# A fused four-stage attention and adapter kernel: three of its TensorE transposes cut into 64-row halves, laid side by side around a group of score products

## The chip, the cores and the metric

The kernel runs on one core of one Trainium2 chip. The metric is the device time of one execution in microseconds (us).

## The reference

For each of 32 samples (256 tokens, 256 features) four residual stages follow each other. Cut to what matters:

```
# stage 1: attention, 16 heads of 16 features; key 0..255 from x, one more key per token from itself
q = (side + b_self) @ Wq + bq;  k = (x + b_prev) @ Wk + bk;  v = x @ Wv + bv
score = q . k / 4, masked beyond the sample's length;  self = q . k_own / 4
w = softmax([score, self]);  attn = w[:-1] @ v + w[-1] * v_own;  x1 = x + attn @ Wo + bo
# stage 2: adapter chosen per sample, layer norm
h = relu(x1 @ W1[id] + b1[id]);  x2 = x1 + layernorm(x1 + h @ W2[id] + b2[id]) * gamma[id] + beta[id]
# stage 3: linear layer chosen per sample
x3 = x2 + x2 @ W3[id].T + b3[id]
# stage 4: pooling with one softmax row per token under a mask chosen per sample
s = tanh(x3 @ W4 + b4) @ v4;  p = softmax(mask(s));  out = x3 + p @ x3 / count
```

## The kernel before

The 32 samples go through a software pipeline: step t computes projections of sample t+2, row maxima of the scores of t+1, the exponentials and weighted values of t, the end of attention of t-1, adapter and linear layer of t-2, pooling of t-3. Steps 6 to 27 are a hardware loop of two steps an iteration; the others are written out. Each engine has its own program in a fixed order, written by hand; semaphores order the engines among each other. There is no scheduler.

TensorE's program of a step is built around eight calls of `scores(pair)`, called S0 to S7 below. Each call issues eight products of 64 rows by 128 columns with 256 moving columns: four write score columns into ST (L584; ScalarE exponentiates them, two "units" a call), four write score rows into SN (L588; VectorE takes the maxima, two units a call). The two kinds lie on different halves of the array's rows (`lo_`, `hi_`) and run side by side. Before it starts, `scores(pair)` waits until the maxima and exponentials of the calls before have been taken. Between the calls stand the other products, almost all of the full array, 128 rows by 128 columns:

- between S1 and S2: `own_keys()` (12 products into bank 2, read by VectorE's `products`, L1386), then `h` (6 products into bank 1);
- between S2 and S3: `queries_back(0)` and `queries_back(1)` (L615): four 128x128 transposes each, of the weighted values `pvt` to token rows in banks `num0` (0) and `num1` (1); then `queries()`;
- between S4 and S5: `own_scores()`, `values("v", ...)`;
- between S5 and S6: `turn(pT, pe3)` and `turn(aT, att)` (L489): four 128x128 transposes each, of the pooling probabilities `pe3` (in `soft`) into bank 1 and of the attention rows `att` (in `nv`) into bank 2; then `weighted(0, ...)` (L563), of 32-column tiles;
- between S6 and S7: `x2T`, the transposes of the normed rows `yn`, then `pool` and `wo`.

A transpose is a product with the data as the stationary operand (its load is a LDWEIGHTS) and the identity (in `fixed`) as the moving one.

`free(name)` waits until the last user of a bank has been read: it walks back through the list `PIECES` (position, name, sample, bank) to the last piece on the same bank, and waits for that piece's entry in `READER`:

```
"h": (("hf", 1, 1),), ... "num0": (("nv", 2, 1),), "num1": (("nv", 2, 2),),
```

So `num1`, on bank 1 behind `h`, waits for `hf`. That is the second of two ScalarE reads of h (L1164 writes `hst`, L1166 writes `hf`). ScalarE's order around it is: units 2 and 3 (L1052), the copy of `pvt` (L1028), the copy of `xs`, `hst`, `hf`, units 4 and 5. Around `pe3` it is: `keys_out` (`kf`), the copy `lwp`, units 8 and 9, the two exponentials of `pe3` with a read of their sums (L1188), the copy `vaug`, units 10 and 11, the copies `p3T` and `aT`, the two `yn` activations (L1206), units 12 and 13. ScalarE and VectorE, like TensorE, take their programs in order.

Of the kernel before, what the change touches and what calls it, by code (L numbers as in the profile page):

```python
# [40 lines left out]
B, S, D = 32, 256, 256  # L41
H, DH = 16, 16
P = 128
NC2 = D // P
# [18 lines left out]


PIECES = [
# [5 lines left out]
]  # L71
# [3 lines left out]
def done(b, per=1, nth=None):  # L75

    nth = per if nth is None else nth
    if isinstance(b, int):
        return 0 if b < 0 else B * per if b >= B else b * per + nth
    return b * per + nth  # L80
# [14 lines left out]
def block4(nc: bass.Bass, x, xsT, lens, ids, wq, wk, wv, wo, wad, lw, lwT, lb, fixed_d, early_d, kidx_d,  # L95
           pmask_d, out):
    ctx = ExitStack()
    with ctx:
# [8 lines left out]
        def sem(name):  # L107
            if name not in sems:
                sems[name] = ctx.enter_context(nc.semaphore(name))
            return sems[name]  # L110
# [7 lines left out]
        ss = [[sb(f"ss{i}{r}", [P, NC2, S], F32R) for r in range(2)] for i in range(2)]  # L118
# [16 lines left out]
        pvt = sb("pvt", [P, 4, S])  # L135
# [3 lines left out]
        att = nv  # L139
# [49 lines left out]
        ident = fixed[:, 2 * H:2 * H + P]  # L189
# [63 lines left out]
        def place(name, t):  # L253

            if isinstance(t, int) and (t, name) in LATE:
                return LATE[t, name][0]
            return place("pool", t) if name == "pool1" else bank[name]
# [40 lines left out]
        def folding(t):  # L298

            return isinstance(t, int) and 0 <= t < 2  # L300
# [174 lines left out]
        def _(pe):  # L475
# [9 lines left out]
            def turn(dst, src):  # L485
# [4 lines left out]
                                                   src[:, i, c * P:c * P + P], ident[:])  # L490
                return last


            pe.wait_ge(sem("hf_set"), 1)
            for _ in range(8):
# [31 lines left out]
            def step(t, par, *only, without=()):  # L527
# [4 lines left out]
                def free(name):  # L532

                    if isinstance(t, int) and (t, name) in LATE:
                        for s, n in LATE[t, name][1]:
                            pe.wait_ge(sem(s), n)
                        return
                    k = NAMES.index(name)
                    mine, u = PIECES[k][3], t
                    while True:  # L540
                        k -= 1
                        if k < 0:
                            k, u = len(PIECES) - 1, u - 1
                        if isinstance(u, int) and u < -2:
                            return
                        _, n, o, on_bank = PIECES[k]
                        if on_bank == mine and folding(u) and n in FOLD:
                            pe.wait_ge(cat, 4 * u + FOLD.index(n) + 1)
                            return
                        if on_bank == mine and (not isinstance(u, int) or 0 <= u + o < B):  # L550
                            for s, per, nth in READER[n]:
                                pe.wait_ge(sem(s), done(u + o, per, nth))
                            return
# [14 lines left out]
                def scores(pair):  # L568

                    if on["C"] and pair % PH == 0:  # L570
                        pe.wait_ge(sem(f"mput{pair // PH}"), done(t, 64))
                    if on["B"] and pair % PH == 0:
                        pe.wait_ge(sem(f"stack{pair // PH}"), done(t + 1, SK))
                    if on["C"]:
                        pe.wait_ge(sem("exp_done"), before(t, 2 * pair))
                    opening = isinstance(t, int) and t == -1
                    rows_to = ST if opening and pair % 2 else SN
                    if on["B"]:
                        pe.wait_ge(sem("maxed"), max(0, 2 * pair - 2) if opening else before(t + 1, 2 * pair))
                    for e in range(2):  # L580
                        lo_, hi_ = 64 * e, 64 * (1 - e)
                        for half in range(2):
                            if on["C"]:
                                keys = nc.tensor.matmul(ST[e][:, half * S:half * S + S],  # L584
                                                        kst[par][lo_:lo_ + MROW + 1, pair, half * P:half * P + P],
                                                        qst[par][lo_:lo_ + MROW + 1, pair, :], start=True, stop=True)
                            if on["B"]:
                                rows_ = nc.tensor.matmul(rows_to[e][:, half * S:half * S + S],  # L588
                                                         qst[odd][hi_:hi_ + MROW, pair, half * P:half * P + P],
                                                         kst[odd][hi_:hi_ + MROW, pair, :], start=True, stop=True)  # L590
                        if on["C"]:
                            keys.then_inc(sem("st_ready"), 1)
                        if on["B"]:
                            rows_.then_inc(sem("sn_ready"), 1)
# [12 lines left out]
                                     lambda r, c: w[r][:, c, :])  # L607
                    last.then_inc(sem(f"{name}_pe"), 1)

                def queries_back(i):  # L610

                    free(f"num{i}")
                    pe.wait_ge(sem("pvt"), done(t - 1, 2))
                    for g in range(4):
                        last = nc.tensor.transpose(place(f"num{i}", t)[:, g * P:g * P + P],  # L615
                                                   pvt[:, g, i * P:i * P + P], ident[:])
                    last.then_inc(sem("num_pe"), 1)

                def linear(i):

# [40 lines left out]
                def own_keys():  # L661

                    free("ks")
                    project("ks", W["k"], ss[odd])
# [59 lines left out]
                scores(1)  # L724
                if first:
                    fold_next("ad")
                elif on["B"]:
                    own_keys()
                if folding(t) and not first:
                    fold_next("h")  # L730
                if go("F", "h"):

                    free("h")
                    pe.wait_ge(sem("x1Thi"), done(t - 2))
                    pe.wait_ge(sem("x1Tlo"), done(t - 2))
                    pe.wait_ge(sem("wlo"), done(t - 2))
                    pe.wait_ge(sem("wsplit"), done(t - 2))
                    three(place("h", t)[:, 0:S], lambda r, c: w1p[r][:, c, :, :].rearrange("p a n -> p (a n)"),
                          lambda r, c: x1T[r][:, c, :]).then_inc(sem("h_pe"), 1)
                scores(2)  # L740
                if go("E", "num"):
                    queries_back(0)
                    queries_back(1)
                if on["A"]:
                    queries()
                scores(3)
# [23 lines left out]
                if on["B"]:  # L770
                    own_scores()
                    free("v")
                    values("v", xs[odd], W["v"])
                scores(5)
                if folding(t):
                    fold_next("pT")
                if go("G", "pT"):
                    free("pT")
                    pe.wait_ge(sem("pe3"), done(t - 3, 2))
                    turn(place("pT", t), pe3).then_inc(sem("pT_pe"), 1)  # L780
                if go("E", "aT"):
                    free("aT")
                    pe.wait_ge(sem("att"), done(t - 1))
                    turn(place("aT", t), att).then_inc(sem("aT_pe"), 1)
# [476 lines left out]
        def _(dve):  # L1261
# [46 lines left out]
            def step(t, par, *only, without=()):  # L1308
# [33 lines left out]
                def numerators(i):  # L1342

                    v4 = place(f"num{i}", t)[:].rearrange("p (h w) -> p h w", w=VW)
                    dve.wait_ge(sem("num_pe"), done(t - 1, 2, i + 1))
                    dve.wait_ge(sem("eself"), done(t - 1))
                    dve.wait_ge(sem("tv"), done(t - 1))
                    dve.wait_ge(sem("aT_pe"), done(t - 2))
                    nc.vector.tensor_tensor(tot[:, i, :], v4[:, :, DH], eself[odd][:, i, :],
                                            ALU.add).then_inc(sem("tot"), 1)  # L1350
                    nc.vector.tensor_tensor(nv[:, i, :].rearrange("p (h d) -> p h d", d=DH), v4[:, :, 0:DH],
                                            tv[odd][:, i, :].rearrange("p (h d) -> p h d", d=DH),
                                            ALU.add).then_inc(sem("nv"), 1)
                    dve.wait_ge(sem("tot"), done(t - 1, 2, i + 1))
                    nc.vector.reciprocal(rec[:, i, :], tot[:, i, :]).then_inc(sem("rec"), 1)  # L1355
# [298 lines left out]
```

## Time and profile before

| | |
|---|---|
| median of 3 runs | 936.23 us (934.44 to 936.3) |
| span of the profiled execution | 933.1 us |
| TensorE matmul busy | 908.0 us, 97% |
| VectorE, ScalarE, GpSimd busy | 74%, 69%, 65% |
| granted TensorE clock, mean | 0.998 of full speed |

The profiled execution's own time stands only as its span, from the first to the last instruction; 3.1 us lie between it and the median, before and behind the span. "PE" is TensorE's products, "PEld" its loads of the stationary operand, "DVE" VectorE, "ACT" ScalarE, "POOL" GpSimd. A product's duration in the trace includes its way through the array, so products that follow each other overlap in the rows; their pace is read from the starts.

### The profile page before, as it was taken

Reading aid. Unit: us, or ns where it says so; the run is one execution under the profiler, and the core shown is the slowest. Engines: PE = TensorE matmul, PEld = TensorE weight load, DVE = VectorE, ACT = ScalarE, POOL = GpSimd, SP = SyncE. Lnnn points to the kernel's source line nnn. Section 1 sums busy time; section 2 is a strip of 40 time slices with the busy share of each in tenths; the row PEclk is TensorE's granted clock in tenths of the full one; section 3 lists DMA queues with packets and bytes.
Section 4 is the critical chain, followed back from the end, with each engine's and each line's share of the span. In section 5 each row is a group of like instructions: output and inputs, shape, how many; then the busy total and the mean of one; then the engine's idle time right before and its main releaser. Section 6 shows DMA issues by size and latency. Waiting matters only on the chain.

```text
span 933.1 us, 27980 instructions
## 1 busy us (share of the span) xinstructions
PE 908.0 (97%) x8611; PEld 760.1 (81%) x8611; DVE 694.6 (74%) x1612; ACT 642.7 (69%) x1381; POOL 602.2 (65%) x767
## 2 busy tenths in 40 slices
PE   8999999999999999999999999999999999999887
PEld 7787888888888888888888888888888888887666
DVE  7766777787777777777778777777877777777555
ACT  4556677777667777767777776777776676776743
POOL 4354767776666776666667666677766667764562
PEclk9999999999999999999999999999999999999999
DMA  7445443444443444544354443344454334433231
GB/s 254 146 139 153 126 129 115 146 143 152 147 129 104 144 135 143 160 133 124 106 160 129 149 154 121 122 126 146 136 156 143 115 125 141 144 115 106 71 95 53
DMA packets 113209, 124.55 MB, mean 133 GB/s; under 512 B 23541, under 2 KB 95110, under 8 KB 113158
## 3 DMA queue, kind: packets, MB, share of 16 engines
q1 hardware_dynamic: 111384, 121.22, 41.5%
q10 hardware_dynamic: 1774, 2.68, 0.9%
q8 instruction: 27, 0.44, 0.2%
q14 instruction: 24, 0.20, 0.1%
HBM read 63.99 MB, written 8.96 MB: 78 GB/s over the span
## 4 chain that ended last, share of the span: by engine, by line
PE 82%; issue 8%; DVE 5%; ACT 3%; POOL 1%; DVEq 1%; POOLq 0%; ACTq 0%
PE M L481 26%; PE ST L584 11%; PE PV L481 10%; PE PV L563 7%; PE M L489 7%; PE SN L588 6%; PE M L803 5%; DVE mx L1335 3%; PE M L615 3%; PE M L673 3%; ACT x1T L1028 2%; PE M L762 2%; PE M L752 1%; PE M L496 1%; ACT pt L1052 0%
## 5 line engine op out<-in xcount | busy, mean ns | idle before, releaser
L1335 DVE TENSOR_REDUCE mx<-SN 128x2 f32<-128x512 f32 x504 | 324.3, 686 | 72.1 <-PE SN L588 72.1
L1052 ACT ACTIVATE pt<-ST 128x512 f32<-128x512 f32 x512 | 277.9, 599 | 78.9 <-PE ST L584 77.2
L584 PE MATMUL ST<-qst,kst 64*128 64x256 f32 x1024 | 187.4, 304 | 9.7 <-DVE mx L1335 4.3
L584 PEld LDWEIGHTS ST<-qst,kst 64*128 64x128 f32 x1024 | 135.9, 185 | 65.3 <-issue 27.2
L588 PE MATMUL SN<-kst,qst 63*128 63x256 f32 x1008 | 183.7, 304 | 0.8 <-issue 0.8
L588 PEld LDWEIGHTS SN<-kst,qst 63*128 63x128 f32 x1008 | 132.6, 185 | 1.4 <-issue 1.0
L563 PE MATMUL PV<-pt,vaug 128*32 128x256 f32 x2048 | 125.1, 385 | 0.1
L887 POOL TENSOR_TENSOR ss<-xsin,ss 128x512 fp32r<-128x512 f32 x32 | 40.9, 1277 | 121.0 <-ACT ss L1028 113.7
L563 PEld LDWEIGHTS PV<-pt,vaug 128*32 128x32 f32 x2048 | 60.4, 110 | 43.7 <-issue 6.4
L481 PE MATMUL M<-lwp,x2T 128*128 128x320 f32 x378 | 68.2, 316 | 1.0 <-issue 1.0
L887 POOL TENSOR_TENSOR x2T<-x2f,x2T 128x512 fp32r<-128x512 f32 x31 | 39.9, 1288 | 42.0 <-ACT x2T L1028 42.0
L887 POOL TENSOR_TENSOR xs<-xsin,xs 128x512 fp32r<-128x512 f32 x31 | 39.8, 1283 | 39.7 <-ACT xs L1028 39.7
L930 POOL TENSOR_TENSOR nv<-nv,rec 128x512 f32<-128x512 f32 x31 | 32.9, 1061 | 42.5 <-DVE rec L1355 42.5
L481 PE MATMUL PV<-Wo,aT 128*128 128x256 f32 x384 | 56.4, 296 | 1.5 <-ACT pvt L1028 1.2
L481 PEld LDWEIGHTS M<-lwp,x2T 128*128 128x128 f32 x378 | 55.9, 189 | 2.1 <-issue 2.0
L803 PE MATMUL M<-x,soft 128*128 128x256 f32 x232 | 54.9, 379 | 0.0
L481 PE MATMUL M<-ss,Wk 128*128 128x256 f32 x384 | 54.2, 290 | 0.0
L481 PE MATMUL PV<-ss,Wq 128*128 128x256 f32 x378 | 52.8, 289 | 1.0 <-POOL ss L887 1.0
L481 PE MATMUL M<-Wv,ss 128*128 128x256 f32 x384 | 53.8, 289 | 0.0
L481 PE MATMUL M<-Wv,xs 128*128 128x256 f32 x384 | 53.5, 289 | 0.1
L481 PEld LDWEIGHTS PV<-Wo,aT 128*128 128x128 f32 x384 | 50.0, 189 | 3.6 <-ACT pvt L1028 1.6
L1028 ACT ACTIVATE kf<-M,bkc 128x256 f32<-128x256 f32 x64 | 26.9, 470 | 35.8 <-PE M L481 35.8
(189 smaller groups left out, 2075.7 us busy)
## 6 DMA issues: line engine op xcount, KB each, us to landing
qst<-qp SPq DMA_DIRECT2D x186, 128.0 KB
kst<-kp SPq DMA_DIRECT2D x186, 128.0 KB
xsin<-in_xsT SPq DMA_DIRECT2D x31, 512.0 KB, 3.4
adw<-in_wad SPq DMA_DIRECT2D x32, 322.5 KB, 3.8
xr<-in_x SPq DMA_DIRECT2D x32, 256.0 KB, 4.1
lwf<-in_lwT SPq DMA_DIRECT2D x32, 256.0 KB, 3.1
pm<-in_pmask SPq DMA_DIRECT2D x31, 257.0 KB, 2.7
out<-ob SPq DMA_DIRECT2D x31, 256.0 KB, 2.2
```

The source lines that it names most:

```text
L481: last = nc.tensor.matmul(dst, left(a, c), right(b, c), start=n == 0, stop=n == 5)
L489: last = nc.tensor.transpose(dst[:, c * S + i * P:c * S + i * P + P], src[:, i, c * P:c * P + P], ident[:])
L563: last = nc.tensor.matmul(PV[32 * j:32 * j + 32, (g % 2) * S:(g % 2) * S + S], vaug[i][:, kb, 4 * g + j, :], pt[:, g, kb, j, :], start=kb ...
L584: keys = nc.tensor.matmul(ST[e][:, half * S:half * S + S], kst[par][lo_:lo_ + MROW + 1, pair, half * P:half * P + P], qst[par][lo_:lo_ + M ...
L588: rows_ = nc.tensor.matmul(rows_to[e][:, half * S:half * S + S], qst[odd][hi_:hi_ + MROW, pair, half * P:half * P + P], kst[odd][hi_:hi_ + ...
L615: last = nc.tensor.transpose(place(f"num{i}", t)[:, g * P:g * P + P], pvt[:, g, i * P:i * P + P], ident[:])
L803: last = nc.tensor.matmul(place(("pool", "pool1")[i], t)[:, i * D:i * D + D], p3T[:, c, i * P:i * P + P], x3_of(t - 3)[:, c, 0:D], start=c ...
L887: return nc.gpsimd.tensor_tensor(dst, src, high.bitcast(F32), ALU.subtract)
L930: nc.gpsimd.tensor_tensor(att[:].rearrange("p c (h d) -> p c h d", d=DH), nv[:].rearrange("p c (h d) -> p c h d", d=DH), rec[:].unsqueeze( ...
L1028: return nc.scalar.activation(dst, src, ACT.Identity, bias=bias)
L1052: nc.scalar.activation(pt[:, g, :, j, :], ST[s % 2][:].rearrange("p (h q) -> p h q", h=2), ACT.Exp, scale=SCALE).then_inc(sem("exp_done"), 1)
L1335: nc.vector.tensor_reduce(out=mx[odd][:, :, 8 * (s // 8) + PH * (1 - s % 2) + s // 2 % PH], in_=(ST if isinstance(t, int) and t == -1 and ...
```

## The change

Each of the three transposes' 128x128 blocks is cut into two halves of 64 rows (`turn_rows`: 64 data rows as the stationary operand, 64 columns of identity moving). Low rows of one block and high rows of another alternate: `num0` with `num1`, `pT` with `aT`. The rest of both blocks follows after a score group, so that two halves for one bank never lie next to each other in time. `queries_back_first` stands ahead of S2 and `queries_back_second` behind it; `pooled_and_rows_first` stands ahead of S5 and `pooled_and_rows_second` behind it. `h` now stands ahead of `own_keys`. Both `free` calls and the wait for the data now stand ahead of a first half, in front of an instruction that only counts up `waited_pe`; a second half waits for the end of its first half. VectorE's `numerators` wait for both blocks at once. The drain steps at the end keep the old whole transposes.

```diff
@@ -63,9 +63,9 @@
 
 
 PIECES = [
-    (0, "pv1", -1, 3), (1, "ks", 1, 2), (1, "h", -2, 1), (2, "num0", -1, 0),
-    (2, "num1", -1, 1), (2, "q", 2, 3), (3, "srep", -3, 2), (3, "ad", -2, 0), (3, "k", 2, 1),
-    (4, "ss", 1, 2), (4, "v", 1, 0), (5, "pT", -3, 1), (5, "aT", -1, 2), 
+    (0, "pv1", -1, 3), (1, "h", -2, 1), (1, "ks", 1, 2), (1, "num0", -1, 0),
+    (1, "num1", -1, 1), (2, "q", 2, 3), (3, "srep", -3, 2), (3, "ad", -2, 0), (3, "k", 2, 1),
+    (4, "ss", 1, 2), (4, "v", 1, 0), (4, "pT", -3, 1), (4, "aT", -1, 2),
     (5, "pv0", 0, 3), (6, "x2T", -2, 1), (6, "pool", -3, 0), (6, "wo", -1, 3), (7, "vs", 1, 2),
     (7, "lin0", -2, 0), (7, "x1T", -1, 2), (7, "lin1", -2, 1),
 ]
@@ -490,6 +490,12 @@
                                                    src[:, i, c * P:c * P + P], ident[:])
                 return last
 
+            def turn_rows(dst, col, src, row_half):
+
+                rows = slice(64 * row_half, 64 * row_half + 64)
+                return nc.tensor.transpose(dst[:, col + 64 * row_half:col + 64 * row_half + 64], src[rows, :],
+                                           ident[rows, rows])
+
 
             pe.wait_ge(sem("hf_set"), 1)
             for _ in range(8):
@@ -607,14 +613,74 @@
                                      lambda r, c: w[r][:, c, :])
                     last.then_inc(sem(f"{name}_pe"), 1)
 
-                def queries_back(i):
-
-                    free(f"num{i}")
+                def queries_back():
+
+                    for i in range(2):
+                        free(f"num{i}")
+                        pe.wait_ge(sem("pvt"), done(t - 1, 2))
+                        for g in range(4):
+                            last = nc.tensor.transpose(place(f"num{i}", t)[:, g * P:g * P + P],
+                                                       pvt[:, g, i * P:i * P + P], ident[:])
+                        last.then_inc(sem("num_pe"), 1)
+
+                def queries_back_first():
+
+                    free("num0")
+                    free("num1")
                     pe.wait_ge(sem("pvt"), done(t - 1, 2))
+                    pe.sem_inc(sem("waited_pe"), 1)
                     for g in range(4):
-                        last = nc.tensor.transpose(place(f"num{i}", t)[:, g * P:g * P + P],
-                                                   pvt[:, g, i * P:i * P + P], ident[:])
-                    last.then_inc(sem("num_pe"), 1)
+                        low_rows = turn_rows(bank["num0"], g * P, pvt[:, g, 0:P], 0)
+                        high_rows = turn_rows(bank["num1"], g * P, pvt[:, g, P:S], 1)
+                    low_rows.then_inc(sem("num_half"), 1)
+                    high_rows.then_inc(sem("num_half"), 1)
+
+                def queries_back_second():
+
+                    pe.wait_ge(sem("num_half"), done(t - 1, 2))
+                    pe.sem_inc(sem("waited_pe"), 1)
+                    for g in range(4):
+                        high_rows = turn_rows(bank["num0"], g * P, pvt[:, g, 0:P], 1)
+                        low_rows = turn_rows(bank["num1"], g * P, pvt[:, g, P:S], 0)
+                    high_rows.then_inc(sem("num_pe"), 1)
+                    low_rows.then_inc(sem("num_pe"), 1)
+
...
+                def pooled_and_rows_first():
+
+                    if go("G", "pT"):
+                        free("pT")
+                    if go("E", "aT"):
+                        free("aT")
+                    if go("G", "pT"):
+                        pe.wait_ge(sem("pe3"), done(t - 3, 2))
+                    if go("E", "aT"):
+                        pe.wait_ge(sem("att"), done(t - 1))
+                    pe.sem_inc(sem("waited_pe"), 1)
+                    for c in range(NC2):
+                        for i in range(2):
+                            if go("G", "pT"):
+                                low_rows = turn_rows(bank["pT"], c * S + i * P, pe3[:, i, c * P:c * P + P], 0)
+                            if go("E", "aT"):
+                                high_rows = turn_rows(bank["aT"], c * S + i * P, att[:, i, c * P:c * P + P], 1)
+                    if go("G", "pT"):
+                        low_rows.then_inc(sem("turn_half"), 1)
+                    if go("E", "aT"):
+                        high_rows.then_inc(sem("turn_half"), 1)
+
+                def pooled_and_rows_second():
+
+                    pe.wait_ge(sem("turn_half"), done(t - 1) + done(t - 3))
+                    pe.sem_inc(sem("waited_pe"), 1)
+                    for c in range(NC2):
+                        for i in range(2):
+                            if go("G", "pT"):
+                                high_rows = turn_rows(bank["pT"], c * S + i * P, pe3[:, i, c * P:c * P + P], 1)
+                            if go("E", "aT"):
+                                low_rows = turn_rows(bank["aT"], c * S + i * P, att[:, i, c * P:c * P + P], 0)
+                    if go("G", "pT"):
+                        high_rows.then_inc(sem("pT_pe"), 1)
+                    if go("E", "aT"):
+                        low_rows.then_inc(sem("aT_pe"), 1)
 
...
@@ -724,8 +790,6 @@
                 scores(1)
                 if first:
                     fold_next("ad")
-                elif on["B"]:
-                    own_keys()
                 if folding(t) and not first:
                     fold_next("h")
                 if go("F", "h"):
@@ -737,10 +801,15 @@
                     pe.wait_ge(sem("wsplit"), done(t - 2))
                     three(place("h", t)[:, 0:S], lambda r, c: w1p[r][:, c, :, :].rearrange("p a n -> p (a n)"),
                           lambda r, c: x1T[r][:, c, :]).then_inc(sem("h_pe"), 1)
+                if on["B"] and not first:
+                    own_keys()
+                if only and go("E", "num"):
+                    queries_back()
+                elif go("E", "num"):
+                    queries_back_first()
                 scores(2)
-                if go("E", "num"):
-                    queries_back(0)
-                    queries_back(1)
+                if not only and go("E", "num"):
+                    queries_back_second()
                 if on["A"]:
                     queries()
                 scores(3)
@@ -771,14 +840,18 @@
                     own_scores()
                     free("v")
                     values("v", xs[odd], W["v"])
+                if not only:
+                    pooled_and_rows_first()
                 scores(5)
+                if not only:
+                    pooled_and_rows_second()
                 if folding(t):
                     fold_next("pT")
-                if go("G", "pT"):
+                if only and go("G", "pT"):
                     free("pT")
                     pe.wait_ge(sem("pe3"), done(t - 3, 2))
                     turn(place("pT", t), pe3).then_inc(sem("pT_pe"), 1)
-                if go("E", "aT"):
+                if only and go("E", "aT"):
                     free("aT")
                     pe.wait_ge(sem("att"), done(t - 1))
                     turn(place("aT", t), att).then_inc(sem("aT_pe"), 1)
@@ -1342,7 +1415,7 @@
                 def numerators(i):
 
                     v4 = place(f"num{i}", t)[:].rearrange("p (h w) -> p h w", w=VW)
-                    dve.wait_ge(sem("num_pe"), done(t - 1, 2, i + 1))
+                    dve.wait_ge(sem("num_pe"), done(t - 1, 2))
                     dve.wait_ge(sem("eself"), done(t - 1))
                     dve.wait_ge(sem("tv"), done(t - 1))
                     dve.wait_ge(sem("aT_pe"), done(t - 2))
```

TensorE, hardware loop, between S1 and S3, before the change (names in brackets are the semaphores waited for; `M` is banks 0 to 2):

```order
L481 MATMUL M<-ss,Wk 128x256 [waits x1bT,x1Tlo]
L481 MATMUL M<-ss,Wk 128x256 x11
L481 MATMUL M<-x1T,w1p 128x256 [waits wlo,x1Tlo,wsplit,x1Thi,x3]
L481 MATMUL M<-x1T,w1p 128x256 x5
L584 MATMUL ST<-qst,kst 128x256 [waits maxed,exp_done]
...
L615 MATMUL M<-fixed,pvt 128x128 [waits pvt,x3]
L615 MATMUL M<-fixed,pvt 128x128 x3
L615 MATMUL M<-fixed,pvt 128x128 [waits pvt,hf]
L615 MATMUL M<-fixed,pvt 128x128 x3
L481 MATMUL PV<-ss,Wq 128x256 [waits ssplit,shi,pvt]
```

The same place with the change (scores are L590 and L594 now, transposes L496):

```order
L481 MATMUL M<-x1T,w1p 128x256 [waits wlo,x1Tlo,wsplit,x1Thi,x3]
L481 MATMUL M<-x1T,w1p 128x256 x5
L481 MATMUL M<-ss,Wk 128x256 [waits x1bT,x1Tlo]
L481 MATMUL M<-ss,Wk 128x256 x11
L496 MATMUL M<-fixed,pvt 128x64 [waits pvt,x3,hf]
L496 MATMUL M<-fixed,pvt 128x64 x7
L590 MATMUL ST<-qst,kst 128x256 [waits maxed,exp_done]
...
L496 MATMUL M<-fixed,pvt 128x64 [waits num_half]
L496 MATMUL M<-fixed,pvt 128x64 x7
L481 MATMUL PV<-ss,Wq 128x256 [waits ssplit,shi,pvt]
```

The wait for `hf` has moved from the fifth transpose behind S2 to the first half transpose ahead of S2.

TensorE, hardware loop, between the value products and `weighted(0)`, before the change:

```order
L481 MATMUL M<-Wv,xs 128x256 x11
L584 MATMUL ST<-qst,kst 128x256 [waits maxed,exp_done]
...
L489 MATMUL M<-fixed,soft 128x128 [waits pe3,kf]
L489 MATMUL M<-fixed,soft 128x128 x3
L489 MATMUL M<-fixed,nv 128x128 [waits att,nself]
L489 MATMUL M<-fixed,nv 128x128 x3
L563 MATMUL PV<-pt,vaug 32x256 [waits qf,v,exp_done]
```

The same place with the change:

```order
L481 MATMUL M<-Wv,xs 128x256 x11
L496 MATMUL M<-fixed,soft 128x64 [waits att,pe3,kf,nself]
L496 MATMUL M<-fixed,nv 128x64
...
L590 MATMUL ST<-qst,kst 128x256 [waits maxed,exp_done]
...
L496 MATMUL M<-fixed,soft 128x64 [waits turn_half]
L496 MATMUL M<-fixed,nv 128x64
...
L569 MATMUL PV<-pt,vaug 32x256 [waits qf,v,exp_done]
```

The waits for `pe3` and `att` have moved from behind S5 to ahead of it.

## Rows read from the trace of the kernel before

**Rows 1.** The page: span, and TensorE's busy time, share, instructions.

```profile
span 933.1 us, 27980 instructions
PE 908.0 (97%) x8611; PEld 760.1 (81%) x8611; DVE 694.6 (74%) x1612; ACT 642.7 (69%) x1381; POOL 602.2 (65%) x767
```

**Rows 2.** Timeline of PE between S1 and S3: start, us, engine, line, operation, tiles.

```profile
462.69 0.38 PE L584 MATMUL ST<-qst,kst 64*128 64x256 f32 x1
...
465.70 0.38 PE L584 MATMUL ST<-qst,kst 64*128 64x256 f32 x1
...
465.92 0.28 PE L584 MATMUL ST<-qst,kst 64*128 64x256 f32 x1
...
466.17 0.27 PE L584 MATMUL ST<-qst,kst 64*128 64x256 f32 x1
466.37 1.21 PE L615 MATMUL M<-fixed,pvt 128*128 128x128 f32 x8
467.33 1.67 PE L481 MATMUL PV<-ss,Wq 128*128 128x256 f32 x12
...
493.87 1.11 PE L615 MATMUL M<-fixed,pvt 128*128 128x128 f32 x8
494.73 1.67 PE L481 MATMUL PV<-ss,Wq 128*128 128x256 f32 x12
```

**Rows 3.** Timeline of PE between S5 and x2T, the same step.

```profile
475.06 0.38 PE L584 MATMUL ST<-qst,kst 64*128 64x256 f32 x1
...
475.72 0.66 PE L489 MATMUL M<-fixed,soft 128*128 128x128 f32 x4
...
476.74 1.93 PE L563 MATMUL PV<-pt,vaug 128*32 128x256 f32 x32
...
479.28 0.66 PE L489 MATMUL M<-fixed,yn 128*128 128x128 f32 x4
```

**Rows 4.** Timelines cut short behind the first, second transpose; and own_scores.

```profile
466.37 0.20 PEld L615 LDWEIGHTS M<-fixed,pvt 128*128 128x128 f32 x2
...
466.37 0.33 PE L615 MATMUL M<-fixed,pvt 128*128 128x128 f32 x1
...
466.37 0.44 PE L615 MATMUL M<-fixed,pvt 128*128 128x128 f32 x2
...
472.54 1.07 PE L673 MATMUL M<-fixed,pr 128*128 128x16 f32 x8
```

**Rows 5.** Timeline of ACT around hf; idle time before an instruction in brackets.

```profile
463.29 1.07 ACT L1052 ACTIVATE pt<-ST 128x512 f32<-128x512 f32 x2
...
464.72 0.64 ACT L1028 ACTIVATE xs<-xsin 128x512 fp32r<-128x512 f32 x1
465.90 0.47 ACT L1164 ACTIVATE hst<-M,adw 128x256 fp32r<-128x256 f32 x1 [0.54 <-PE M L481]
466.40 0.47 ACT L1166 ACTIVATE hf<-M,adw 64x256 f32<-64x256 f32 x1
```

**Rows 6.** Timeline of ACT from kf to yn.

```profile
471.97 0.84 ACT L1028 ACTIVATE kf<-M,bkc 128x256 f32<-128x256 f32 x2 [1.12 <-PE M L481]
...
475.17 0.21 ACT L1188 ACTIVATION_READ_ACCUMULATOR soft<-soft,nm 128x1 f32 x1
...
475.74 1.10 ACT L1052 ACTIVATE pt<-ST 128x512 f32<-128x512 f32 x2
...
477.65 1.15 ACT L1206 ACTIVATE yn<-y,shift,rstd 128x256 f32<-128x256 f32 x2
```

**Rows 7.** Timelines of DVE and PEld: two releases of S1, and an idle time.

```profile
461.35 1.29 DVE L1335 TENSOR_REDUCE mx<-SN 128x2 f32<-128x512 f32 x2
...
131.56 1.28 DVE L1335 TENSOR_REDUCE mx<-SN 128x2 f32<-128x512 f32 x2
...
132.96 0.18 PEld L584 LDWEIGHTS ST<-qst,kst 64*128 64x128 f32 x1 [0.63 <-issue]
...
469.51 1.29 DVE L1335 TENSOR_REDUCE mx<-SN 128x2 f32<-128x512 f32 x2 [0.66 <-PE SN L588]
```

## The prediction, as it was put on record

> **What bounds the kernel now.** I read the page first: TensorE has products in flight for 97% of the span [rows 1], every other engine at most 74%. So what lies on TensorE's program decides. Then the timeline of TensorE through one step. The first `pvt` transpose starts at 466.37 in one step and at 493.87 in the next [rows 2], so a step lasts 27.50 us, and some 30 such steps (32 samples and the pipeline's ends) make up the span. The reader is to see that the rows follow each other almost without a gap; the largest stall left is ahead of S1, where 462.69 follows the end of two maxima at 461.35 + 1.29 = 462.64 [rows 2, 7]. Then ScalarE's timeline around the two places of the change. It shows something that TensorE's rows don't: when the data become ready that the moved waits ask for.
>
> **What the halves can give.** A whole transpose takes 0.11 us: cut behind the first and the second, the products of L615 span 0.33 and 0.44 [rows 4]. A half has 64 moving columns in place of 128, so 0.055. Its load still has 128 columns. Of the first two loads, 0.14 each, the pair spans 0.20 [rows 4], so the second started 0.06 behind the first. Loads in the other half of the rows run beside these, as the score products show: of two kinds, one pair starts each (466.17 - 465.92) / 2 = 0.12 us [rows 2]. So I take 0.06 for a pair of halves, and this has no row of its own: the trace has no transpose of 64 rows. From above it is bounded by 0.11, the pace of whole transposes and also that of the loads of `own_scores`: eight products with 16 moving columns in 1.07, the last lasting about 0.27, hence (1.07 - 0.27) / 7 = 0.11 [rows 4]. From below by 0.055. I take the value near the low end, since transposes' own loads show 0.06.
>
> Here a rule speaks against the change. The Trainium skill, "TensorE: Matmul & The Clock Gate", LDWEIGHTS (loading the stationary operand), says that the load time goes by the columns alone, and that 32 rows take as long as 128; as an estimate from its figure, 128 columns take 107 ns. By that a pair of halves would cost as much as a whole transpose and the sum would be that of the second rival below. The trace agrees for ordinary products and disagrees for transposes, whose loads start 0.06 apart.
>
> The chain from the first half to what follows is then: 4 pairs of halves 0.24, the load of the first score product 0.11, 4 score pairs 0.48, 4 pairs 0.24, and 0.09 for the change back to whole tiles: the last score product starts at 466.17, the first transpose 0.20 later [rows 2], of which 0.11 are the product itself. Together 1.16. Before, from the start of S2 to the query products it is 467.33 - 465.70 = 1.63, and in every other step 0.10 less (494.73 - 493.87 = 0.86 against 0.96) [rows 2], in the mean 1.58. From the start of S5 to `weighted` it is 476.74 - 475.06 = 1.68 [rows 3]. With no new wait the change would give 0.42 + 0.52 = 0.94 us a step.
>
> **First moved wait: hf.** The first halves want to start where S2 starts now, at 465.70, since swapping `h` and `own_keys` moves 18 products but not their sum. They wait for `hf`. ScalarE ends `hf` now at 466.40 + 0.47 = 466.87 [rows 5]. It sat idle for 0.54 before `hst`, waiting for h, and that wait goes since h comes earlier. Behind the copy of `xs` (464.72 + 0.64 = 465.36) `hst` can start at once, or, as instructions on ScalarE overlap by some 0.10 (`kf`, two like `hst` at 0.47 each, takes 0.84) [rows 5, 6], 0.64 earlier than now. I take 0.60: `hf` ends at 466.27. ScalarE can't be earlier: its units 2 and 3 start 0.60 behind S1 (462.69 to 463.29) [rows 2, 5] and it has no other idle time up to `hst`. TensorE's release costs 0.05 where the waiting instruction is the load itself (462.64 to 462.69), and 131.56 + 1.28 = 132.84 to 132.96, hence 0.12, where the wait stands in the queue ahead of it [rows 2, 7]. Here it stands on the instruction ahead, so 0.12. First half at 466.39, queries at 466.39 + 1.16 = 467.55, against 465.70 + 1.58 = 467.28: **+0.27 us**. The stall of 0.69 eats the gain of 0.42.
>
> Behind TensorE in this stall wait the score rows of S2, 0.9 later than now (0.69 and the 0.24 of halves). VectorE takes them late, with `numerators` behind; it has 0.66 of idle time before unit 6 [rows 7], and unit 6 itself moves by 0.27. So that is just covered. `products` reads `ks` later by the six products of h, ahead of the same units, and adds nothing.
>
> **Second moved wait: pe3.** The first halves want to start at 475.06. `pe3` ends at 475.17 + 0.21 = 475.38 [rows 6], and ScalarE has had work without idle time from `kf` at 471.97 on, which TensorE's own keys release, so it moves with TensorE. With 0.12 the first half starts at 475.50. S5 starts 0.24 later, at 475.74, which is 0.68 later than now. `weighted` could start at 475.50 + 1.16 = 476.66, 0.08 earlier than now. But S5 also feeds ScalarE's units 10 and 11. By the 0.60 seen at S1 they start at 476.34 instead of 475.74, and `p3T`, `aT` and `yn` stand behind them without a gap; `yn` ends at 477.65 + 1.15 = 478.80 now and at 479.40 then. The `x2T` transposes start at 479.28 now [rows 3], with slack; then at 479.40 + 0.05 = 479.45: **+0.17 us**. So this stall is passed on through ScalarE, and what TensorE had saved is lost waiting for `yn`.
>
> `att` is no concern: POOL forms it right behind the numerators, before S4, and it is used at S5. The 16 more transposes a step are in the 0.06. The second halves wait for the end of their first, which lies a whole score group back. I cost that at nothing; if S5's or S2's 0.48 did not cover a product's way through the array, it would be some 0.1.
>
> **Sum.** 0.27 + 0.17 = 0.44 us a step, times 30 steps that have both (h from step 2 on, pe3 from step 3): +13 us. The profiled span of 933.1 becomes 946, and with the 3.1 us around it, as in the median of 936.23, **949 us**. Bounds within this case: `hf` 0.04 earlier and a release of 0.05 give 0.16 + 0.10, +8 us; `hf` 0.06 later and one more queue instruction of 0.1 at each place (the next score group's waits stand in the queue too, which was full before and is empty after a stall) give 0.43 + 0.27, +21 us. Range 944 to 957.
>
> **Rivals.**
>
> Second, the halves run at 0.11 a pair. The chain is 0.44 + 0.11 + 0.48 + 0.44 + 0.09 = 1.56. First place 466.39 + 1.56 - 467.28 = +0.67. At the second, S5 starts at 475.94 and `yn` gives +0.37 (TensorE's own +0.32). 1.04 x 30 = +31 us: **967 us**. For it: loads of 128 columns elsewhere take 0.11 [rows 4], and no row shows a 64-row transpose. Against: the transposes' loads.
>
> Third, on the other side: the moved waits don't bind, because ScalarE is earlier than I think at both places. The place is `hf` ready by 465.70 and `pe3` by 475.06. Then the change does what its shape promises, 0.94 x 30 = -28 us: **908 us**. Each 0.1 us of stall that is missing at both places gives back some 6 us, and the time crosses that of now when the stalls are together 0.44 shorter (`hf` about 0.27 earlier, and `pe3` 0.17). Against it: ScalarE's rows are packed from the release by TensorE to the end of `hf` and of `pe3`, and its program isn't touched.
>
> Fourth, stalls and gains cancel within 0.2%: the lower bounds above and a little more overlap of halves and scores, **936 us**.
>
> **Chances.** The forecast 0.56, the second 0.18, the third with all that is partly so 0.15, the fourth 0.09; the last 0.02 go to VectorE being later than its idle time and still more loss. A measurement of this kernel tells about 0.2%, 2 us, from no change. So faster 0.15, same 0.09, slower 0.76. The range takes in the cancelling case and some of each outer one: 932 to 965.
>
> **What would show it.** In the changed profile: a PE idle time ahead of the first halves of `pvt`, released by ACT `hf`, near 0.5 to 0.7 us from S1 + 3.01; one ahead of the halves of `soft` released by ACT L1188, near 0.4; `x2T` waiting for `yn`; ACT's idle time before `hst` gone; eight halves of L496 spanning some 0.5 with their way through the array if pairs take 0.06, and 0.7 if they take 0.11; a step of 27.9 us. No idle time ahead of the halves would make the forecast wrong in sign, halves at 0.11 in size.

## The result

The changed kernel takes 957.46 us (956.21 to 958.69, 4 runs) against 935.34 us (934.11 to 936.3, 4 runs) for the kernel before: ratio 1.024, 95% interval 1.0227 to 1.0253, 22 us more. The forecast was 949, within 932 to 965, and slower.

The page of the changed kernel, its span, busy times and chain by engine; they answer to [rows 1]. The last line is the same chain in the kernel before:

```profile
span 954.5 us, 29064 instructions
PE 888.0 (93%) x9099; PEld 747.6 (78%) x9099; DVE 717.7 (75%) x1612; ACT 640.3 (67%) x1381; POOL 601.5 (63%) x767
...
PE 61%; issue 16%; ACT 14%; DVE 5%; POOL 1%; SPq 1%; DVEq 1%; ACTq 0%; DMA 0%; POOLq 0%
...
PE 82%; issue 8%; DVE 5%; ACT 3%; POOL 1%; DVEq 1%; POOLq 0%; ACTq 0%
```

TensorE has 20 us less work in flight, as intended, and the span is 21 us longer. ScalarE has 14% of the chain that ended last, where it had 3%. So the work did shrink, and waits took its place.

The timeline of PE between S1 and S3, in a step of the loop; it answers to [rows 2]:

```profile
471.94 0.38 PE L590 MATMUL ST<-qst,kst 64*128 64x256 f32 x1
...
473.41 1.59 PE L481 MATMUL M<-ss,Wk 128*128 128x256 f32 x12
475.86 0.46 PE L496 MATMUL M<-fixed,pvt 64*128 64x64 f32 x8 [0.86 <-ACT hf L1239]
476.10 0.36 PE L590 MATMUL ST<-qst,kst 64*128 64x256 f32 x1
...
476.66 0.43 PE L496 MATMUL M<-fixed,pvt 64*128 64x64 f32 x8
477.02 1.69 PE L481 MATMUL PV<-ss,Wq 128*128 128x256 f32 x12
```

Before the change, the next step's S1 and S2, beside the rows of [rows 2]:

```profile
490.20 0.38 PE L584 MATMUL ST<-qst,kst 64*128 64x256 f32 x1
...
493.19 0.38 PE L584 MATMUL ST<-qst,kst 64*128 64x256 f32 x1
```

The reader is to see two things. From the first half to the queries it is 477.02 - 475.86 = 1.16 us, against 1.63 and 1.54 from S2 to the queries before: the halves give what they should. But they start 3.92 behind S1 (471.94) where S2 started 3.01 or 2.99 behind it, so queries stand 5.08 behind S1 instead of 4.64 or 4.53. The idle time in brackets names `hf`.

ScalarE in the same step, around hf; it answers to [rows 5]:

```profile
473.97 0.64 ACT L1101 ACTIVATE xs<-xsin 128x512 fp32r<-128x512 f32 x1
474.49 0.48 ACT L1237 ACTIVATE hst<-M,adw 128x256 fp32r<-128x256 f32 x1
475.00 0.47 ACT L1239 ACTIVATE hf<-M,adw 64x256 f32<-64x256 f32 x1
```

The idle time before `hst` is gone. `hf` ends at 475.47, 3.53 behind S1. The first half starts 0.39 after that.

The second place, PE from S4 on, and ScalarE beside it; these answer to [rows 3] and [rows 6]:

```profile
481.57 0.38 PE L590 MATMUL ST<-qst,kst 64*128 64x256 f32 x1
...
485.31 0.24 PE L496 MATMUL M<-fixed,soft 64*128 64x64 f32 x1 [0.48 <-issue]
485.31 0.27 PE L496 MATMUL M<-fixed,nv 64*128 64x64 f32 x1
485.39 0.22 PE L496 MATMUL M<-fixed,soft 64*128 64x64 f32 x1
...
485.52 0.22 PE L496 MATMUL M<-fixed,soft 64*128 64x64 f32 x1
...
486.48 1.93 PE L569 MATMUL PV<-pt,vaug 128*32 128x256 f32 x32
...
489.16 0.66 PE L489 MATMUL M<-fixed,yn 128*128 128x128 f32 x4
```

```profile
484.88 0.21 ACT L1261 ACTIVATION_READ_ACCUMULATOR soft<-soft,nm 128x1 f32 x1
...
486.07 1.09 ACT L1125 ACTIVATE pt<-ST 128x512 f32<-128x512 f32 x2 [0.48 <-PE ST L590]
...
488.00 1.11 ACT L1279 ACTIVATE yn<-y,shift,rstd 128x256 f32<-128x256 f32 x2
```

`pe3` ends at 485.09 and the halves start at 485.31. The profile puts that wait down to "issue", but the end of ScalarE's L1261 stands just ahead of it; `att`, the other data waited for there, is ready at 480.43 already by POOL's row (its spans are rough). To `weighted` it is 1.17 again. ScalarE's new idle time of 0.48 before its units carries the lateness on to `yn` (its end is 489.11), and `x2T` starts right behind, at 489.16. A step of the hardware loop is 28.18 us long instead of 27.48 (mean distance between the `x2T` transposes of 21 steps in a row).

The written-out steps are not so much longer: 27.94 instead of 27.50 in two of them. Their rows, of one such step in the changed kernel, PE and ScalarE:

```profile
134.30 0.35 PE L590 MATMUL ST<-qst,kst 64*128 64x256 f32 x1 [0.17 <-DVE mx L1408]
...
137.86 0.46 PE L496 MATMUL M<-fixed,pvt 64*128 64x64 f32 x8 [0.50 <-issue]
```

```profile
137.29 0.47 ACT L1239 ACTIVATE hf<-M,adw 64x256 f32<-64x256 f32 x1
```

Here the first half follows 0.10 after the end of `hf` (137.76), and so it does in all eight written-out steps that have it. In the 22 steps of the loop it follows after 0.34 to 0.43.

### The profile page after: what moved, and what is told of

Read it like the earlier page. It is cut to its first block, busy times and chain, and to the rows that moved or that the text cites. A ratio compares the mean times of both kernels' runs of the same rounds, so it can differ in the third digit from the quotient of the medians.

```text
span 954.5 us, 29064 instructions
## 1 busy us (share of the span) xinstructions
PE 888.0 (93%) x9099; PEld 747.6 (78%) x9099; DVE 717.7 (75%) x1612; ACT 640.3 (67%) x1381; POOL 601.5 (63%) x767
## 4 chain that ended last, share of the span: by engine, by line
PE 61%; issue 16%; ACT 14%; DVE 5%; POOL 1%; SPq 1%; DVEq 1%; ACTq 0%; DMA 0%; POOLq 0%
PE M L481 19%; PE PV L481 10%; PE ST L590 7%; PE M L876 5%; PE M L496 4%; PE SN L594 4%; PE M L489 4%; PE M L739 3%; ACT yn L1279 3%; ACT pt L1125 3%; DVE mx L1408 3%; ACT aT L1101 2%; ACT x1T L1101 2%; PE M L831 2%; PE PV L569 2%
## 5 line engine op out<-in xcount | busy, mean ns | idle before, releaser
L590 PE MATMUL ST<-qst,kst 64*128 64x256 f32 x1024 | 189.5, 306 | 8.2 <-DVE mx L1408 5.2
L590 PEld LDWEIGHTS ST<-qst,kst 64*128 64x128 f32 x1024 | 139.1, 188 | 55.3 <-issue 27.0
L594 PE MATMUL SN<-kst,qst 63*128 63x256 f32 x1008 | 180.9, 304 | 0.8 <-issue 0.8
L594 PEld LDWEIGHTS SN<-kst,qst 63*128 63x128 f32 x1008 | 131.3, 187 | 1.4 <-issue 0.9
L1459 DVE SCALAR_TENSOR_TENSOR pr<-M,bsc,qf 128x256 f32<-128x256 f32 x64 | 28.0, 479 | 37.4 <-PE M L481 37.4
L1440 DVE TENSOR_TENSOR x<-M,lbr 128x320 f32<-128x320 f32 x60 | 29.2, 486 | 34.7 <-PE M L481 34.7
```

The costliest lines, as they stand in the source:

```text
L590: keys = nc.tensor.matmul(ST[e][:, half * S:half * S + S], kst[par][lo_:lo_ + MROW + 1, pair, half * P:half * P + P], qst[par][lo_:lo_ + M ...
```

## Experiments

All ratios are to the kernel before, timed beside it.

**Each place alone.** In the first run `h`, `own_keys` and the numerators are as before the change, in the second the pooled probabilities and attention rows:

```diff
+                elif on["B"]:
+                    own_keys()
...
-                if on["B"] and not first:
-                    own_keys()
-                if only and go("E", "num"):
+                scores(2)
+                if go("E", "num"):
                     queries_back()
-                elif go("E", "num"):
-                    queries_back_first()
-                scores(2)
-                if not only and go("E", "num"):
-                    queries_back_second()
...
```

```diff
-                if not only:
-                    pooled_and_rows_first()
                 scores(5)
-                if not only:
-                    pooled_and_rows_second()
...
```

> Only the pooled probabilities and attention rows are in halves; numerators, h and own_keys stand as before the change. Theory (each place loses by its own wait on ScalarE; the changed profile shows step +0.69 us, of which S4 to x2T is 7.59 against 7.41): step +0.18, times 29, about +5 us, ratio to the kernel before 1.006. Rival (the loss is in the array or the queue, by the number of half transposes, which is the same at both places): half of the loss, +11 us, 1.012.

> Only the numerators are in halves, with h ahead of own_keys; pooled probabilities and attention rows are whole behind S5. Theory: step +0.50, +15 us, 1.016, PE idle ahead of the halves of pvt released by hf, near 0.9. Rival (by number of halves): +11 us, 1.012.

Measured: 942.15 us, 1.0065 (1.0047 to 1.0084), and 949.68 us, 1.015 (1.0131 to 1.0169). The two add up to 20 of the 22 us. The same number of half transposes costs 6 us at one place and 14 at the other, each as its own wait would have it. The rival of both expectations, 11 us each by the number of halves, falls.

**The swap alone**, whole transposes:

```diff
-                elif on["B"]:
-                    own_keys()
...
+                if on["B"] and not first:
+                    own_keys()
                 scores(2)
```

> The kernel before with h ahead of own_keys and nothing else. Theory: hf ends some 0.6 earlier, the fifth whole transpose no longer waits for it (0.1 in every other step), products read ks later under cover: 0 to -2 us, 0.998 to 1.000. Rival (the later ks is what costs, through VectorE's maxima): +10 us or more, 1.01.

Measured: 934.86 us, 0.9995 (0.9985 to 1.0005). The later `ks` costs nothing. In its profile `hf` and the whole transposes stand so:

```profile
465.60 0.47 ACT L1166 ACTIVATE hf<-M,adw 64x256 f32<-64x256 f32 x1
```

```profile
466.20 1.09 PE L615 MATMUL M<-fixed,pvt 128*128 128x128 f32 x8
467.05 1.67 PE L481 MATMUL PV<-ss,Wq 128*128 128x256 f32 x12
```

`hf` ends ahead of all eight, so the wait of 0.1 between the two blocks is gone too.

**The order of the waits.**

```diff
+                    pe.wait_ge(sem("pvt"), done(t - 1, 2))
                     free("num0")
                     free("num1")
-                    pe.wait_ge(sem("pvt"), done(t - 1, 2))
                     pe.sem_inc(sem("waited_pe"), 1)
```

> The changed kernel with the wait for pvt ahead of the two waits for the banks of the numerators, so that the wait for hf is the last one ahead of the halves. Theory (after hf is released two more queue instructions, 0.25 us in all, stand ahead of the first half): they are passed before the wait, the step is 0.15 to 0.25 shorter, -5 to -7 us against the changed kernel, 1.017 to 1.019 of the kernel before. Rival (the time from the end of hf to the first load is the way of the semaphore alone): no change, 1.024.

Measured: 953.27 us, 1.0183 (1.0163 to 1.0203), and a step of the loop 0.27 shorter than in the changed kernel. Its rows, PE and ScalarE, in the loop and then in a written-out step:

```profile
470.29 0.38 PE L590 MATMUL ST<-qst,kst 64*128 64x256 f32 x1
...
473.91 0.46 PE L496 MATMUL M<-fixed,pvt 64*128 64x64 f32 x8 [0.57 <-issue]
```

```profile
473.34 0.47 ACT L1239 ACTIVATE hf<-M,adw 64x256 f32<-64x256 f32 x1
```

```profile
138.61 0.46 PE L496 MATMUL M<-fixed,pvt 64*128 64x64 f32 x8 [0.65 <-ACT hf L1239]
```

```profile
137.88 0.47 ACT L1239 ACTIVATE hf<-M,adw 64x256 f32<-64x256 f32 x1
```

`hf` ends 3.52 behind S1, as in the changed kernel (3.53), but the first half follows 0.10 after it, not 0.39. So in the loop 0.3 of this stall hung on the order of the waits, 0.27 a step in the mean. In the written-out steps the same edit works the other way: the first half follows 0.26 after `hf` there (138.61 - 138.35) where it was 0.10, and the two steps of 27.94 and 27.97 take 28.10 and 28.11. Nor does a wait behind the released one always cost 0.3: behind the wait for `pe3` the wait for `att` and the counting instruction stand in the same way, and the half follows in 0.22, in the loop and outside it. The waits take their counts from the loop's counter in one case and from constants in the other; whether that is the reason was not tested, and what TensorE's queue does in these 0.3 us stays open.

**The data earlier.** Both are moves on ScalarE, which leave TensorE's program alone:

```diff
                 if go("E", "pvt1"):
                     groups(t - 1, 1)
-                if on["A"]:
-                    other_high()
                 if go("F", "h"):
...
+                if on["A"]:
+                    other_high()
                 unit(4)
```

```diff
-                if go("F", "lwhi"):
...
                         nc.scalar.activation(yn[:, i, :], y[:, i, :], ACT.Identity, scale=rstd[:, i:i + 1],
                                              bias=shift[:, i:i + 1]).then_inc(sem("normed"), 1)
+                if go("F", "lwhi"):
...
                 unit(12)
```

> The changed kernel with ScalarE's two reads of h ahead of its copy of xs, so that hf ends some 0.5 us earlier. Theory (the halves wait 0.9 us a step for hf): the idle time ahead of the halves of pvt falls to some 0.4, 0.5 times 30 = -15 us against the changed kernel, 942 us, 1.007 of the kernel before. Rival (something else holds the halves there, such as pvt, or the time comes back before S3): no change, 1.024.

> The changed kernel with ScalarE's copy lwp moved from ahead of units 8 and 9 to behind yn, so that pe3 ends 0.63 earlier. Theory: the wait of 0.55 ahead of the halves of soft goes, S5 starts on time, yn ends some 0.45 earlier: -13 us against the changed kernel, 944 us, 1.010. Rival (the lower part of the linear weights, formed by POOL behind lwp, comes late for lin0 and takes the place of the wait): 1.02 or more.

> The changed kernel with hf earlier, pe3 earlier and the wait for hf last in the queue. Theory (the halves are worth 0.94 us a step where their data are there): -0.52 - 0.45 - 0.22 = -1.2 a step against the changed kernel, 36 us: 921 us, 0.984 of the kernel before. Rival (the gain of the halves is lost elsewhere whatever their waits): not under 1.000.

Measured: 942.77 us, 1.0083 (1.0066 to 1.01); 941.77 us, 1.0083 (1.0063 to 1.0102); and with both and the wait for `hf` last 924.32 us, 0.9878 (0.9858 to 0.9898). Each move alone shortens the step of the loop by 0.52. With both and the order of the waits it is 26.89, which is 0.59 under the kernel before. The last one's PE and ScalarE, around the two places:

```profile
465.27 0.38 PE L590 MATMUL ST<-qst,kst 64*128 64x256 f32 x1
...
468.45 0.27 PE L496 MATMUL M<-fixed,soft 64*128 64x64 f32 x1
...
469.62 1.93 PE L569 MATMUL PV<-pt,vaug 128*32 128x256 f32 x32
...
472.33 0.66 PE L489 MATMUL M<-fixed,yn 128*128 128x128 f32 x4
...
483.27 0.38 PE L590 MATMUL ST<-qst,kst 64*128 64x256 f32 x1
...
486.38 0.46 PE L496 MATMUL M<-fixed,pvt 64*128 64x64 f32 x8
...
487.55 1.69 PE L481 MATMUL PV<-ss,Wq 128*128 128x256 f32 x12
```

```profile
467.95 0.22 ACT L1256 ACTIVATION_READ_ACCUMULATOR soft<-soft,nm 128x1 f32 x1
...
471.17 1.11 ACT L1274 ACTIVATE yn<-y,shift,rstd 128x256 f32<-128x256 f32 x2
```

The halves of `soft` start 3.18 behind S4, where S5 stood before the change (475.06 - 471.87 = 3.19), and those of `pvt` 3.11 behind S1, 0.1 late. `x2T` is now 7.06 behind S4 against 7.59 in the changed kernel. It still follows `yn`, which ends at 472.28.

A control has the same two moves on the kernel before:

> The kernel before (whole transposes) with only the two moves on ScalarE: the two reads of h ahead of the copy of xs, the copy lwp behind yn. Theory (these moves give time only where halves wait for hf and pe3): 0 to -3 us, 0.997 to 1.000 (yn ends earlier, but x2T doesn't wait for it). Rival (the moves are what made the version with both earlier fast): -8 us or more, 0.991 or less.

Measured: 937.78 us, 1.0029 (1.0016 to 1.0041). Without halves to wait for their results, the moves cost 3 us, and both expectations missed the sign. A step of the loop is 0.09 longer. Where that comes from is open: TensorE's idle time ahead of the `weighted` loads is 7.1 us in the whole span here and in the kernel before. The gain of the version with both is then the halves', since the moves alone give none.

**Are halves side by side?**

```diff
-                        high_rows = turn_rows(bank["num1"], g * P, pvt[:, g, P:S], 1)
+                        high_rows = turn_rows(bank["num1"], g * P, pvt[:, g, P:S], 0)
```

and likewise at the three other places.

> The changed kernel with the low rows of both blocks ahead of the score group and the high rows of both behind it, so that no two halves in a row lie on different rows of the array. Theory (halves on different rows run side by side, 0.06 a pair; on the same rows 0.06 each): each group of eight takes 0.24 longer, 0.48 at the first place and some 0.33 at the second, +24 us against the changed kernel, 981 us, 1.05. Rival (halves don't run side by side, 0.03 is the queue's pace for any): no change, 1.024.

Measured: 975.68 us, 1.0435 (1.0417 to 1.0452). The halves of `soft` and `nv` in its PE timeline:

```profile
496.18 0.25 PE L496 MATMUL M<-fixed,soft 64*128 64x64 f32 x1 [0.48 <-issue]
496.27 0.22 PE L496 MATMUL M<-fixed,nv 64*128 64x64 f32 x1
...
496.39 0.23 PE L496 MATMUL M<-fixed,nv 64*128 64x64 f32 x1
...
496.53 0.38 PE L594 MATMUL SN<-kst,qst 63*128 63x256 f32 x1
...
497.69 1.93 PE L569 MATMUL PV<-pt,vaug 128*32 128x256 f32 x32
```

On the same rows each half takes 0.06 (two in 496.39 - 496.27 = 0.12), on different rows a pair takes that (two pairs in 485.52 - 485.39 = 0.13 in the changed kernel). From the first half to `weighted` it is 1.51 instead of 1.17, 0.34 more and not 0.48, since the first score product starts at 496.53, ahead of the last two halves. So the expected 981 was a little high.

**The last steps.** The version with both, with whole transposes in the last three full steps:

```diff
+                whole = bool(only) or (isinstance(t, int) and t >= B - 3)
...
-                if not only:
+                if not whole:
                     pooled_and_rows_first()
```

> The version with hf and pe3 earlier, with whole transposes in the last three full steps. That version's last steps ran 5 us longer than those of the kernel before, with half the clock granted for 14 us more. Theory (the gaps ahead of the halves and the thinner work of the halves in these steps, where the projections of new samples are missing, let the clock fall): the clock stays, -4 us against that version, 920 us, 0.984. Rival (the clock falls in the last steps for another reason): 924 us or more, 0.988, and the same stretches at half clock.

Measured: 921.88 us, 0.9854 (0.9838 to 0.9871). Against 0.9878 with halves throughout the intervals overlap, so the two aren't told apart by their times. From 830 to 860 and from 860 to 890 the mean granted clock was 0.94 and 0.89 of full speed, and 0.89 and 0.77 in the version with halves throughout. From the first to the last `x2T` its profiled execution is 2.8 us shorter; ahead of the first one it lost 2.5, where this edit changes nothing and where its clock had fallen to 0.91 between 20 and 40. That the clock falls less at the end with whole transposes there fits the theory, but it is one trace of each.

## Why the prediction was right, step by step

The forecast's mechanism is what the runs show, and its size is 13 us where 22 were measured. The parts that make up the difference are these:

- **What bounds the kernel**: TensorE's program, with ScalarE deciding when moved waits are released. It held, with 61% of the chain on TensorE, though ScalarE's share grew to 14%.
- **The chain of 1.16 us** from first half to what follows, and with it the pace of 0.06 a pair: 1.16 and 1.17 measured. The second rival, 0.11 a pair, is out. The halves' loads in the changed kernel, PEld:

```profile
485.34 0.14 PEld L496 LDWEIGHTS M<-fixed,soft 64*128 64x128 f32 x1
485.37 0.14 PEld L496 LDWEIGHTS M<-fixed,nv 64*128 64x128 f32 x1
485.40 0.14 PEld L496 LDWEIGHTS M<-fixed,soft 64*128 64x128 f32 x1
```

Loads of the same rows start 0.06 apart. The rule that load time goes by columns, in the Trainium skill, "TensorE: Matmul & The Clock Gate", LDWEIGHTS (loading the stationary operand), does not fit transposes here: that is about half of the 107 ns which, as an estimate, its figure gives for 128 columns.

- **The first moved wait** was right in kind, and its size is the term that was off. The end of `hf` was taken 3.58 behind S1 (466.27 - 462.69) and measured at 3.53. The release was taken at 0.12, "Here it stands on the instruction ahead", with 0.22 as the far bound, and measured 0.39 in this step of the loop. The wait for `hf` was not the last one: the one for `pvt` and the counting instruction came behind it. With the order turned it is 0.10 in the loop. So the place cost 0.50 (5.08 against the mean of 4.64 and 4.53), not 0.27. The row from which the 0.12 was read (132.84 to 132.96) lies in a written-out step, and in those the release does take 0.10.
- **The second moved wait**: +0.17 forecast, and 7.59 - 7.41 = +0.18 measured from S4 to `x2T` (the 7.41 is 479.28 - 471.87 in the profile of before). The first half came 0.22 behind `pe3`, not 0.12, yet the way the stall was passed on, through units 10 and 11 to `yn`, was as described.
- **Sum**: 0.44 a step forecast, 0.70 measured in the loop. The prediction had one price for 30 steps. In the traces the 22 distances that end in a step of the loop add 15.4 us, five written-out ones 0.40 to 0.47 each, 2.2 together, the last three 2.9, and 0.9 come ahead of the first `x2T`. The written-out steps match the forecast 0.44, in part by luck: with each place alone they are 0.19 and 0.25 longer, where the prediction had 0.27 and 0.17. The 2.9 at the end had no term in the sum; the last section has the clock there.
- **VectorE** just covered its lateness: in the changed kernel its maxima behind S3 start at 479.22 with no idle time before them, where it had 0.66 [rows 7]. That `products` reads `ks` later costs nothing, as the swap alone shows.
- **The third rival**, that the waits don't bind, was wrong for the change, and its 28 us are too many even with the data nearly on time: the ratio is 0.9878 then, 11 us under the kernel before. Of the 0.94 a step promised, 0.59 came in the loop. `yn` on ScalarE holds `x2T`, which is the rest of the second place, and 0.1 of stall is left at the first.

## What to carry to other kernels

When work is moved ahead of where it stood, look up on the other engine when its data are ready, counted from the same event, before counting what the work itself saves; here an expected gain of 0.94 us a step met first halves that could start only 0.91 (3.92 - 3.01) and 0.55 (3.74 - 3.19) later behind the score group ahead. If several waits stand ahead of an instruction, try their order, and read it in loop steps and written-out steps apart: with the one that ends last put last, the loop's steps won 0.27 here and the written-out ones lost some 0.15. And a neighbour engine's order is part of such a change: the halves lost 22 us with ScalarE's order as it was and gained 11 with two of its operations moved and the wait for `hf` put last, while the same two moves alone lost 3.

## What was not expected of the hardware

From the end of a released producer to the first half it took 0.39 us with one more wait and the counting instruction behind the released wait, and 0.10 with that wait last. That is so in the loop's steps; in the written-out ones the two orders took 0.10 and 0.26.

The granted clock fell near the end of several runs. The same two steps, from `x2T` to `x2T`, without projections of new samples, in the kernel before and then in the version with both moves; columns are the stretch, its length, busy us and count by engine, PE clock, DMA share, GB/s:

```profile
836.48:862.58 26.10, 24.77 (x242) 20.22 (x240) 20.51 (x50) 17.53 (x38) 12.05 (x19) 1.00 0.30 95
862.58:887.39 24.81, 21.00 (x183) 15.28 (x181) 12.63 (x32) 16.89 (x36) 14.55 (x20) 0.93 0.22 67
```

```profile
822.28:851.24 28.96, 26.60 (x256) 22.41 (x257) 20.64 (x50) 17.43 (x38) 12.63 (x18) 0.88 0.28 86
851.24:878.64 27.40, 22.43 (x196) 16.91 (x197) 12.11 (x32) 17.41 (x37) 13.52 (x19) 0.75 0.20 61
```

A mean of 0.75 is half of that stretch at 1.2 GHz, the lower level. In the version with both, 30 steps shorter by 0.59 would be 18 us, but its span is only 933.1 - 924.5 = 8.6 us shorter. The traces say where the rest is: from the first `x2T` on, the distances up to the last three save 14.7 us, the last three give 5.6 back, and 0.5 go ahead of the first `x2T`. The length of the first of the two steps goes with its mean clock in all twelve traces: 26.1 and 26.4 us at 1.00 (the kernel before and the swap alone), 27.0 to 28.1 at 0.94 (seven kernels, the changed one with 27.3 among them), 28.7 to 29.0 at 0.88 (`hf` waited last, `hf` earlier, both earlier). So most of the 5.6 us is probably time at the lower clock, and so is part of the changed kernel's 2.9. No run changed the clock alone. What makes it fall was not settled: from 100 to 795 us its mean is 1.00 in the kernel before, the changed kernel and the version with both alike, and the two moves on the kernel before, with no halves at all, bring 0.94 in this step too.
